# Four shared-expert tiles read from on-chip buffers, and four re-orderings, in a fused adaLN + state + mixture-of-experts kernel

## The reference, cut to what matters

```python
mod = (silu(c) @ wmod)                       # sa, ca, ga, sb, cb, gb, each of 512 columns
h = layernorm(x) * (1 + ca) + sa             # x: 2048 tokens x 512
x = x + ga * (tanh(h @ B.T) @ C.T + D * h)
h = layernorm(x) * (1 + cb) + sb
# mixture of experts: 8 experts of width 352, top 2 by sigmoid score + bias
y = sum over the 2 experts of w * (silu(h @ W1) * (h @ W3)) @ W2
y = y + shared expert of width 704           # (silu(h @ sw1.T) * (h @ sw3.T)) @ sw2.T
out = x + gb * y
```

## Time and profile before

| | us |
|---|---|
| three runs: median (lowest to highest) | 570.36 (569.66 to 571.24) |
| the profiled execution: its own time | 571.33 |
| its span, first to last instruction | 569.7 |
| mean granted TensorE clock | 0.990 of full |

### The profile page before, as it was taken

The page is one execution under the profiler, slowest core; times in us unless marked ns, Lnnn a source line. Parts: engine busy times, 40 slices in busy tenths (PEclk is TensorE's granted clock), DMA queues, the critical chain, the costliest instruction groups (busy, mean ns, idle before and its releaser), DMA issues.

```text
span 569.7 us, 11068 instructions
## 1 busy us (share of the span) xinstructions
PE 543.4 (95%) x3129; PEld 487.3 (86%) x3130; DVE 286.6 (50%) x612; ACT 176.3 (31%) x337; POOL 263.5 (46%) x221
## 2 busy tenths in 40 slices
PE   8996899999999995999999999999999999988997
PEld 3665788998999894999999999999999999987896
DVE  3788586686687565442222222222222222158897
ACT  1444345445534330122223222322223223112211
POOL 2599877668666457343016260044443300254630
PEclk9999899999999998999999999999999999999999
DMA  8999266543452889566254946255758313475982
GB/s 309 395 337 382 84 212 249 186 160 116 166 191 106 286 316 375 190 220 227 96 161 157 326 138 231 74 175 192 288 167 310 129 55 110 152 257 188 314 306 79
DMA packets 47915, 119.80 MB, mean 210 GB/s; under 512 B 4752, under 2 KB 5008, under 8 KB 47888
## 3 DMA queue, kind: packets, MB, share of 16 engines
q1 hardware_dynamic: 35088, 67.02, 33.4%
q0 software_dynamic: 12800, 52.43, 26.0%
HBM read 80.38 MB, written 39.06 MB: 210 GB/s over the span
## 4 chain that ended last, share of the span: by engine, by line
PE 79%; POOL 7%; issue 5%; DMA 4%; DVE 3%; ACT 1%; SPq 0%; POOLq 0%; DVEq 0%; ACTq 0%
PE bank L1007 14%; PE bank L1009 14%; PE bank L1008 14%; PE bank L1038 8%; PE bank L1040 7%; PE bank L1039 7%; PE bank L984 4%; PE bank L1045 4%; PE bank L955 2%; PE bank L953 2%; PE bank L954 2%; DMA x_all<-wmod 2%; POOL tmpa L595 1%; DMA xt_low<-xal 1%; POOL x_all L598 1%
## 5 line engine op out<-in xcount | busy, mean ns | idle before, releaser
L1007 PE MATMUL bank<-whi,thi 128*128 (+1 forms) x416 | 139.9, 336 | 8.3 <-issue 8.3
L1008 PE MATMUL bank<-wlo,thi 128*128 (+1 forms) x416 | 135.9, 327 | 0.0
L1009 PE MATMUL bank<-whi,tlo 128*128 (+1 forms) x416 | 135.5, 326 | 0.0
L582 POOL TENSOR_TENSOR wlo<-raw,whi 128x1408 f32 (+3 forms) x24 | 79.6, 3329 | 83.7 <-DMA whi<-w_all 74.0
L1007 PEld LDWEIGHTS bank<-whi,thi 128*128 128x128 f32 x416 | 79.5, 191 | 9.0 <-issue 9.0
L1742 DVE TENSOR_TENSOR gbuf<-s,bank 128x352 f32<-128x352 f32 x52 | 27.0, 520 | 112.5 <-ACT s L927 111.5
L1038 PE MATMUL bank<-whi,gth 128*128 (+1 forms) x201 | 79.9, 397 | 2.3 <-DVE gtl L1305 1.3
L1040 PE MATMUL bank<-whi,gtl 128*128 (+1 forms) x201 | 79.0, 393 | 0.0
L1008 PEld LDWEIGHTS bank<-wlo,thi 128*128 128x128 f32 x416 | 79.0, 190 | 0.0
L1009 PEld LDWEIGHTS bank<-whi,tlo 128*128 128x128 f32 x416 | 78.9, 190 | 0.0
L1039 PE MATMUL bank<-wlo,gth 128*128 (+1 forms) x201 | 78.8, 392 | 0.0
(11 more groups left out here) (222 smaller groups left out, 951.8 us busy)
## 6 DMA issues: line engine op xcount, KB each, us to landing
raw<-w_all POOLq DMA_DIRECT2D x8, 2176.0 KB
whi<-w_all POOLq DMA_DIRECT2D x16, 704.0 KB, 11.5
h<-xs_rows SPq DMA_DIRECT2D x36, 256.0 KB, 2.7
ys_rows<-tmpa SPq DMA_DIRECT2D x36, 256.0 KB, 2.0
x_all<-wmod SPq DMA_DIRECT2D x6, 1024.0 KB, 9.7
whi<-w_all POOLq DMA_DIRECT2D x8, 768.0 KB, 4.6
hs_rows<-h SPq DMA_DIRECT2D x8, 512.0 KB, 5.1
xt_high<-xah SPq DMA_DIRECT2D x8, 512.0 KB
```

The source lines that it names most:

```text
L582: pool.tensor_tensor(wlo[:, bass.ds(off + (SH + a), b - a)], raw[:, a:b], whi[:, bass.ds(off + (SH + a), b - a)].bitcast(F32), ALU.subtrac ...
L1007: pe.matmul(dst, xh[:, j, a], wh, start=(m == 0), stop=False)
L1008: pe.matmul(dst, xh[:, j, a], wl, start=False, stop=False)
L1009: mm = pe.matmul(dst, xl[:, j, a], wh, start=False, stop=(m == KD - 1))
```

## The change

- B takes the **last** four tiles. The pair 6 stays in `xah`/`xal` and the pair 7 is split into `xbh`/`xbl`, so neither is stored to DRAM and nothing is loaded for B. C then takes tiles 0 to 11, and every index of tiles, weights and outputs moves with it. C's tiles are loaded into four places (`xah`, `xbh` with both halves), four tiles deep, the first two during S.
- The split of pair 7 no longer waits for the store of pair 6; DVE waits there for `s_stp` of the last pair. `gtl` of the last step moves from `xah` to `shi`/`slo`.
- Body 3 on POOL: both roots come ahead of `with_d(2)`. Body 3 on DVE: the first statistics come behind `gbuf` (L1301), and `gtl` (`low_a`) comes ahead of both h2 operations.
- Stage C: the first gathers for a combined tile are issued one place earlier, `weigh` stands behind the copy of `gth` and at k = 2, 4, 5, 7, 8, 10, and the parts of `combine` follow `COMBINE_AT`; the very last part comes behind `finish_last(0)`. PE's loop in C is unrolled.

```diff
-FIRST_LAST = [*range(NB), *range(NT - NL, NT)]
-WEIGH_AT = [3, 4, 6, 7, 9, 10]
+NC = NT - NB
+FIRST_LAST = [*range(NC, NT), *range(NC - NL, NC)]
+WEIGH_AT = [2, 4, 5, 7, 8, 10]
+COMBINE_AT = [(), (), (), (0, 1), (2,), (3, 4), (5, 6), (7, 8), (9, 10), (11, 12), (13, 14), (15, 16)]
...
-        gth_b, gtl_b = xah[:, 0, 0:FP], xah[:, 1, 0:FP]
+        gth_b, gtl_b = (t[:, :, :].rearrange("p a b -> p (a b)")[:, 0:FP] for t in (shi, slo))
+        xt_place = [(xah, xal, 0), (xah, xal, 1), (xbh, xbl, 0), (xbh, xbl, 1)]
...
-                if live(3, lo, hi):
+                if live(3, lo, hi) and lo <= NP:
                     store_x(it - 3)
...
-                if k < NT - NB:
-                    sp.wait_ge(q["S", "up"], iters * 2 + (NB + k - 1))
-                    load_x(NB + k, k % 2)
+                if k < NC:
+                    sp.wait_ge(q["S", "up"], iters * 2 + (NB + k - 3))
+                    load_x(k)
...
-            for t in range(2, NB):
-                sp.wait_ge(q["S", "up"], t - 1)
-                load_x(t, t % 2)
-            sp.wait_ge(s_xts, 32 * NP)
...
             store_y(0, 0)
+            sp.wait_ge(s_xts, 32 * (NP - 2))
+            sp.wait_ge(q["S", "up"], 2)
+            for t in range(2):
+                load_x(t)
...
+                if lo == 3:
+                    with_d(2)
                 if lo > 2 and live(0, lo, hi):
                     times_d(it)
...
                     pool.wait_ge(w_ready, 2 * NW)
-                    for t in range(2):
-                        pool.wait_ge(q["C", "xin"][t], 32)
                     fetch_raw(0)
...
             times_d(2)
-            with_d(2)
             iterations(pool, body, 3)
...
+            for k in range(2):
+                gather_first(0, k)
...
+                if lo > 3 and not (lo == NP + 1 and p == NP - 1):
                     act.wait_ge(s_xts, p * 32)
+                dst = xbh if lo == NP + 1 and p == NP - 1 else xah
...
-            iters = steps(pe, step, lambda: pairs_of_b(pe))
+            iters = steps(pe, step, lambda: pairs_of_b(pe), True)
...
                 if lo == 3:
+                    first_stats(it, lo)
+                    first_aggr(it, lo)
                     first_weights(2)
                 between(1)
+                if lo == 3:
+                    low_a(it - 3, 0, lo)
...
                     finish_last(0, 0, 1)
+                    combine(NB + NL - 1, 2)
```

More of the change, by code:

```diff
@@ L247, in build @@
         s_xts = sem("s_xts")
+        s_xl = [sem(f"s_xl{b}") for b in range(4)]
         s_lg = sem("s_lg")
@@ L266, in build @@
                 q[sec, n] = sem(f"{n}_{sec}")
-            q[sec, "xin"] = [sem(f"xin{j}_{sec}") for j in range(2)]
+            if sec == "S":
+                q[sec, "xin"] = [sem(f"xin{j}_{sec}") for j in range(2)]
             q[sec, "ydma"] = [sem(f"ydma{j}_{sec}") for j in range(2)]
@@ L416, in rows_of_pair, with load_x @@
                              ).then_inc(s_hrow[b], 16)
-            def load_x(t, j):
-                for dst, src in ((xbh, xth), (xbl, xtl)):
-                    sp.dma_start(dst[:, j, :].bitcast(F32), src[t * P:(t + 1) * P, :]).then_inc(q["C", "xin"][j], 16)
+            def load_x(t):
+                high_, low_, j = xt_place[t % 4]
+                for dst, src in ((high_, xth), (low_, xtl)):
+                    sp.dma_start(dst[:, j, :].bitcast(F32), src[t * P:(t + 1) * P, :]).then_inc(s_xl[t % 4], 16)
             def store_x(p):
@@ L510, in _ @@
             for j in range(2):
-                next_c(j)
+                next_c(j + 2)
                 store_y(iters + (j - 2), 1 - j)
@@ L515, in _ @@
                     k = (c - CB) * 2 + j
-                    next_c(k + 2)
+                    next_c(k + 4)
                     if k == 0:
@@ L529, in _ @@
                     sp.wait_ge(s_ly[t], h + 1)
-                    sp.dma_start(out[(NT - NL + t) * P:(NT - NL + t + 1) * P, w],
+                    sp.dma_start(out[(NC - NL + t) * P:(NC - NL + t + 1) * P, w],
                                  rowb[NB + t][:, 1, w]).then_inc(s_lout, 16)
@@ L936, in step @@
                 act.activation(gth_b if last else gth[:, :], bank[4][:, 0:FP], ACT.Copy).then_inc(q["S", "ghi"], 1)
+                if k in WEIGH_AT:
+                    weigh(WEIGH_AT.index(k))
                 if (sec == "S" and not (isinstance(i, int) and i + j == CB)) or (sec == "C" and isinstance(c, int) and c + j == CB):
@@ L988, in up @@
                 xh, xl = (xah, xal) if sec == "A" else (xbh, xbl)
+                if sec == "A" and isinstance(i, int) and i == NP - 1:
+                    xh, xl = xbh, xbl
                 if loaded is not None:
-                    pe.wait_ge(q["C", "xin"][j], loaded * 32)
+                    xh, xl = xt_place[loaded % 4][0:2]
+                    if loaded >= 4:
+                        pe.wait_ge(s_xl[loaded % 4], 32 * (loaded // 4))
+                    else:
+                        pe.wait_ge(q["A", "xlo"], NT)
                 elif sec == "A":
@@ L1229, in step @@
                 up("S", i, j, off, [NW + 1, NW + 2] if sec == "B" else need_up,
-                   i + 1 if sec == "B" else c + 1 if sec == "C" else None, last)
+                   i * 2 + j if sec == "B" else 4 + (c - CB) * 2 + j if sec == "C" else None, last)
                 if first:
@@ L1469, in lows_a @@
             def lows_a(p, lo):
+                high_, low_ = xah, xal
+                if lo == NP + 1 and p == NP - 1:
+                    dve.wait_ge(s_stp, NP)
+                    high_, low_ = xbh, xbl
                 for j in range(2):
                     dve.wait_ge(q["A", "xhi"], p * 2 + (j + 1))
-                    dve.tensor_tensor(xal[:, j, :], h2_bank(lo, j)[:, :], xah[:, j, :].bitcast(F32),
+                    dve.tensor_tensor(low_[:, j, :], h2_bank(lo, j)[:, :], high_[:, j, :].bitcast(F32),
                                       ALU.subtract).then_inc(q["A", "xlo"], 1)
@@ L1511, in body @@
                         dve.tensor_tensor(xt, bank[j][:, :], xt, ALU.add).then_inc(s_x1, 1)
-                if live(0, lo, hi) and lo != 2:
+                if live(0, lo, hi) and lo not in (2, 3):
                     first_stats(it, lo)
@@ L1522, in body @@
                 if live(0, lo, hi):
-                    if lo != 2:
+                    if lo not in (2, 3):
                         first_aggr(it, lo)
@@ L1573, in body @@
                     between(5, 6)
-                if live(3, lo, hi):
+                if live(3, lo, hi) and lo > 3:
                     low_a(it - 3, 0, lo)
@@ L1659, in routed @@
                 link(dve.tensor_tensor(pos[:, :, :], pos[:, :, :], yp, ALU.add))
-                for t, n, a in ((0, NB, 0), (NB, NL, NT - NL)):
+                for t, n, a in ((0, NB, NC), (NB, NL, NC - NL)):
                     dve.tensor_copy(idxb[:, 2 * t:2 * t + 2 * n].rearrange("p (t k) -> p t k", k=2),
@@ L1711, in finish @@
                     dve.wait_ge(q["C", "ydma"][j], (c - CB) * 16)
-                w = [wts[:, c * 2 + j:c * 2 + j + 1, k] for k in range(2)]
+                w = [wts[:, n - 1:n, k] for k in range(2)]
                 dve.scalar_tensor_tensor(y, tbuf[:, j, :], w[0], bank[5 + j][:, :],
@@ L1748, in step @@
                 if m >= 0:
-                    for n in range(2 * m, 2 * m + 2):
+                    for n in COMBINE_AT[m + 3]:
                         combine(n // 3, n % 3)
```

22 lines of the change are left out of this document (7 added, 15 removed).

## The result

The changed kernel takes **564.7 us** (median of 4 runs, 563.0 to 565.4), the kernel before 570.0 in the same runs (569.7 to 571.2): ratio 0.989, interval 0.987 to 0.992. It is faster by 1.1%, a third of what I forecast (554.0), and outside my range. The profiled execution took 565.4 us, and its span is 563.7, which is 5.9 less than that of before.

A forecast was written before the change was run, and what follows sets the result against it. PE, busy 543.4 of 569.7 us, was taken as the bound, so only its idle or slow spots could win. 8.9 + 1.3 + 2.4 + 4.4 - 0.6 = 16.4 us off the median 570.36 gave 554.0, range 551 to 560.

The forecast's parts named there:

- part 4: Stage C: four-deep loads, earlier gathers and weigh behind gth remove three PE waits in the 10.67 us step; 4.4 us won.
- rival C: Stage C: the stall only moves, ACT held by weigh or DVE's slack too small; 558.4 us, chance 0.10.
- Part 1: Pause at 219 us before B's third tile: no tile load, so 6.45 us plus 2.4 of half clock; 8.9 won.
- rival D: Pause at 219 us isn't the tile load, so its 8.9 us stay; 562.9 us, chance 0.03.
- Rival A: Last B step: scattered rows come late, so PE waits for the first expert tile; 561.3 us, chance 0.12.
- Part 2: PE's wait for xal at 192.93: the split no longer waits for pair 6's store; 1.3 us won.
- Part 3: Opening, body 3: earlier gtl and roots bring the next h2 transposes forward; 2.4 us won.
- rival B: Opening gives nothing, as POOL's sums slow DVE and delay the second tile's g; 556.4 us, chance 0.12.
- the 68.9 of my working: Opening: forecast start time in us of body 4's h2 transposes, against 71.28 before.
- The end: Last DVE chain: one combine part (0.69) moves behind finish_last(0); 0.6 us lost.
- Rival E: Stage C: PE's unrolled code is fetched through full DMA queues, making the kernel slower; 579.8 us, chance 0.02.

The follow-up runs named there:

- e4: Kernel before, with the twelve gathers of the first and last tiles' results as plain DMAs from fixed rows: ratio 0.996 to before.
- c4: Changed kernel, with the twelve extra indirect gathers replaced by plain POOL DMAs of the same size: 556.5 us, ratio 0.973 to before.
- e1: Changed kernel; extra gathers wait on combined tiles (tile n: s_c2 >= n + 2), weigh and combine parts a step later, with_d(2) behind slo: 555.1 us, ratio 0.972.
- c2: Kernel before, with only the change's new stage C schedule of gathers, weigh and combine parts: 574.8 us, ratio 1.004.
- c3: Kernel before, with only PE's loop over stage C unrolled: ratio 0.998 to before.
- d3: c1 with the opening undone (with_d(2), statistics and gtl at their old places): ratio 0.986 to before.
- c1: Changed kernel, with the old stage C schedule of the twelve extra gathers, weigh and combine parts: 562.9 us, ratio 0.984 to before.
- e2: e1 with the extra gathers released one combined tile earlier (tile n: s_c2 >= n + 1): ratio 0.984 to before.
- e3: e2 without its waits ahead of the extra gathers, so POOL's first row is 10 again: ratio 0.990 to before.
- d4: c1 with with_d(2) on POOL held until DVE's slo of body 3 is done: ratio 0.982 to before.
- d1_paced: Changed kernel, with tighter waits on POOL's stage C gathers, each tile's held until the tile before is combined: ratio 1.017 to before.

## Why the prediction was wrong

**The step that failed is part 4, stage C.** I wrote that gathers one place earlier would take the 1.00 us behind `gtl` away and "the same gathers and parts are spread over the same steps, so I count no new stall". The first two gathers of the extra tiles went directly behind the four that open the stage. That made one row of ten, and PE's completion signals came up to 6.25 us late; two rows of eight followed, the last with a signal 3.19 late and the lower clock behind it. Forecast 4.4 won, measured 4.06 lost: 8.5 of the 10.5 us by which the forecast missed in the profiled execution. My rival C had the place, but its price was "the stall only moves", no gain and no loss; I had put no price on what a fuller POOL does to others. The trace of before held the sign: its rows of 8 had late signals too (1.34 at 525.4). I had read the releasers by name and not asked when the releasing work had ended. In the long step of the earlier trace rows the largest delay was 0.45, so as far as the trace shows its three waits were what I had taken them for, the tile load and the gather. The parts of the sum inside were right where they could be tested alone: the tile load is real (e4), and once the rows are short all three waits go and stage C takes 74.1 (c4, e1), 5.3 under before, 0.9 more than the 4.4 I had put.

**Part 1, the pause.** Right for this execution, 8.9 us with the clock (PE's turn of g is 2.65 us ahead of before's in front of the pause and 11.55 behind it), and rival D is false. Rival A too: no idle row ahead of the first expert's turn but 0.32, since SP's load of the scattered rows moved from 227.99 to 219.01. But the term was one execution's. c2, c3 and e4 have the same code there and paused for 4.79, 5.00 and 4.68 us instead of 6.45; the end of S stands at 480.7 to 481.2 in them and at 482.7 in the profiled one. So of the 8.9 the usual gain is nearer to 7. What I left out: in the last B step DVE's L1661 now runs beside POOL's low parts and takes 2.48 us, 0.42 before, and `gbuf` is 0.38 late. With a few small rows about 1.1 us.

**Part 2, pair 7.** Right: the idle 1.28 at 192.93 is gone. This term too was one execution's: the same wait took 0.67, 0.86 and 1.01 us in c2, c3 and e4.

**Part 3, the opening.** 2.4 forecast, 1.28 measured (1.2 by d3 against c1): half of rival B. I had read the collision of POOL's sums with DVE and thought that DVE had 5 us to spare; the sums met two operations, which lost 4.2 us, while the pair that they had met before (L1549, 3.46 us) fell to 1.40. The Trainium skill (GPSIMD Engine Reference, Specifications) states the shared interfaces, and the row agrees: L1585 has two SBUF tensors as inputs and goes from 1.41 to 3.44. With the sums behind `slo`, and the clock as low and for as long as in the kernel before, e2 and e3 start the transposes at 68.85 and 68.73: the 68.9 of my working. With the full clock from the start e1 has 67.16.

**The end.** 0.6 lost was forecast, 0.4 measured.

**Rival E.** False as far as tried (c3, and no long step in e1, whose code is unrolled). The Trainium skill (Advanced Engine Details and Errata, ISA Cache) gives two cache lines of 256 instructions, but also 128KB on TensorE where the other engines have 32KB, which my prediction left out; no run here shows a price for it.

**Shown and open.** That the gathers make the signals late is shown by making twelve of them plain (c4), by spreading them (e1), and by adding a row of 10 alone (c2). Each of the three rows of 10 gave delays of over 6 us. Length alone is not the whole rule: rows of 8 gave 0.5 to 3.5 us, and pairs of rows of 4 with 0.79 between gave up to 2.0 in c1, none in e1. Why PE's signals wait, and whether it is the indirection or POOL's time under it, is open; c4 changes both.

## What to carry to other kernels

When work is moved earlier on an engine that issues DMAs, count how many now stand in a row, and look at other engines' waits in that stretch: a wait whose releasing work had long ended can be a late signal, as here, and not missing work. Move a gather to where it is wanted by a wait on a consumer one tile back, and check in the trace that the wait really leaves a pause; waits that also held the main gathers cost 16 us against the changed kernel, and holding the extra ones a tile less cost 7 against e1. And a pause in a full queue varies from one execution to the next (4.7 to 6.5 us in four profiled executions), so a term read from it needs a range.

## What the runs showed that I had not expected

- Signals of PE that reach the semaphore 1 to 6.5 us after the matmuls ended, while POOL issues eight or ten indirect gathers in a row.
- An indirect gather of 128 rows of 2 KB holds POOL for 0.94 to 1.5 us, with 0.30 to the next one, and the rows of three of them land 5.1 to 6.3 us after their start in the chain of d1_paced. A plain DMA of the same size holds it for 0.6.
- The idle time behind a late signal can cost PE's clock too: 0.50 was granted behind 2.21 us of idle in the changed kernel, but 1.00 stayed behind the 3.03 us before it.
- After the same idle 3.3 us in the opening the granted clock was 1.00 in e1 and d3, at half (1.2 GHz) until about 60 us in before, after, c1, e2 and e3, and until 62 in d4. The start of h2's transposes is 1.6 to 2.7 us earlier in e1 than in e2, e3 and d4, whose opening is the same; so a part of e1's lead over them (its S ends 1.8 us earlier than e2's) is that clock, in the profiled execution.
